# Fewer, larger instructions for the high and low parts of the probabilities in a cross-attention kernel

## Chip, cores and metric

The kernel runs on 1 core of one Trainium2 chip. The metric is device time in microseconds (us), from launch to end, of one execution. The kernel before took a median of 1032.5 us over 3 runs (1031.4, 1032.5 and 1037.69 us). The profiled execution is a further one.

## What is computed

Four batches of 2048 tokens with 640 channels attend to 77 context rows of 1024 numbers: the first 73 are text (T = 73), the last 4 are image-prompt rows. There are 20 heads of 32 channels. The reference, cut to what matters:

```python
q = heads(hidden_states @ W_q)
scores_t = jnp.einsum('bhsd,bhtd->bhst', q, k_t) * attn_scale
probs_t = jax.nn.softmax(scores_t, axis=-1)
text_out = jnp.einsum('bhst,bhtd->bhsd', probs_t, v_t)
attn_scores = jnp.einsum('bhsd,bhnd->bhsn', q, k_ip) * attn_scale
qsem = _l2norm(jnp.einsum('bhst,bte->bhse', probs_t, text_ehs))
sem = jnp.einsum('bhse,bne->bhsn', qsem, ip_n)
probs_ip = jax.nn.softmax(attn_scores + 0.5 * sem, axis=-1) * spatial_mask
ip_out = jnp.einsum('bhsn,bhnd->bhsd', probs_ip, v_ip)
out = (text_out + ip_out) @ W_out + b_out + residual
```

## The kernel before

A prologue prepares weights and per-batch tables (about the first 90 us). Then `main_loop` runs over 160 **pairs**. A pair is 256 tokens (2 blocks of 128, index j) of one group of 4 heads (HG = 4). Two pairs make a slot (512 tokens, 4 heads), five slots make a tile (512 tokens, all 20 heads), and there are 16 tiles. Each engine has its own loop over p, written out by hand; the engines meet only at semaphores. Within step p:

- TensorE (PE): the scores of pair p into `ps_S` (L1122); at times transposes of x for a later tile into `ps_M` (L1138); pieces of the output projection of the tile before into `ps_O` (L1164, the table `OUT_AT`); the product of the probabilities of pair p - 2 (LU = 2) with the table `xm` into `ps_U` (L1184), which needs the transposed probabilities `pts`; a part of the query projection of a later slot into `ps_Q` (L1198).
- VectorE (DVE): the maximum of the scores (`smax`, L1014), a copy of the image-prompt scores (`s_ip`, L1017), the exponent's bias (`bias`, L1021), low parts of queries and x (L994), then the work on pair p - 2: norms, reciprocals, `attn` (L1046 to L1102). It adds the output projection to x (L1006).
- ScalarE (ACT): copies out of PSUM (`qT` L868, `xT` L874), `at16` (L896), then for pair p eight exponentials of 73 columns (`pr`, L905), and the **high parts** (L917).
- GpSimd (POOL): three Newton steps every second pair (L944 to L950), the low part of the attention output (`at16`, L961), mask and weights of the image-prompt part (L969, L976), and the **low parts** of pair p (L987), last in its step.
- SyncE's queue (SP): in step p first the loads of tables (`kbd` L785, `xm` L795) and stores and loads of x (L801, L807), then the two DMA transposes of pair p (L825), then that of a slot's attention output (L841). All of these stand in one queue, in this order.

The probabilities go to the matmul of L1184 as two float16 numbers, a high part hi = f16(p) and a low part lo = f16(p - hi), that lie side by side as contraction rows. For each head `ph` has 256 columns: hi in 0 to 72, lo in 73 to 145, hi once more in 146 to 218 (the third piece meets the low part of the other operand), the rest is zero. Seen as `[P, 2, HG, 2, P]`, this is two tiles of 128 columns, and the low parts cross the border between them: SPLIT = 55 of them lie in the first tile, LO_B = 18 in the second. So before, ScalarE writes hi with two instructions for each j (`for col in (0, P + LO_B)`, 4 heads x 73 = 292 elements each), the semaphore `ph_ready` rises with the second, and GpSimd makes lo with two subtractions, of 4 x 55 = 220 and of 4 x 18 = 72 elements. `pl_ready` counts these: 4 for each pair. The transposes (L825) wait for `ph_ready` and `pl_ready`; so does the VectorE product (L1060), which overwrites `pr`.

`ph` and `pts` have rings of 2, `pr` one of 3. ScalarE waits before it writes `ph` until the transpose of pair p - 2 has landed; the transposes of pair p wait (L821) until TensorE has read `pts` of pair p - 2.

Of the kernel before, what the change touches and what calls it, by code (L numbers as in the profile page):

```python
# [9 lines left out]
ALU = mybir.AluOpType  # L10
ACT = mybir.ActivationFunctionType
# [7 lines left out]
HG = 4  # L19
# [604 lines left out]
def main_loop(nc, top, g):  # L624

    P, B, S, C, T, T_ALL, CC = (g[k] for k in "P B S C T T_ALL CC".split())
    XW, COL_G, COL_ONE, COL_V, IPR, HALF, DH, SPLIT = (
        g[k] for k in "XW COL_G COL_ONE COL_V IPR HALF DH SPLIT".split())
# [11 lines left out]
    X_RING, XT_RING, AT_RING, P_RING, SIP_RING, PH_RING, PT_RING = NI, 8, 10, 3, 3, 2, 2  # L640
# [4 lines left out]
    LO_B = T - SPLIT  # L645
# [9 lines left out]
    def sb(name, shape, dt):  # L655
        return top.enter_context(nc.sbuf_tensor(name, shape, dt))

    def sem(name):
        return top.enter_context(nc.semaphore(name))
# [10 lines left out]
    pr = [sb(f"pr{i}", [P, 2, HG, T], F32) for i in range(P_RING)]  # L670
    ph = [sb(f"ph{i}", [P, 2, HG, 2, P], F16) for i in range(PH_RING)]
# [23 lines left out]
    p_ready, ph_ready, pl_ready = sem("p_ready"), sem("ph_ready"), sem("pl_ready")  # L695
# [28 lines left out]
    def pair_of(p):  # L724
        return p if 0 <= p < PAIRS else None

    def slot_of(n):
        return n // 2 if n % 2 == 0 and 0 <= n // 2 < ALL_SLOTS else None

    def q_at(p):  # L730

        part = (p + 1) % 2
        m = slot_of(p + 3 - part)
        return None if m is None else (m, part)

    def x_at(p):

        if p == FIRST:
            return [(0, c) for c in range(CC)]
        return [(j, c) for at, c in XT_AT.items() for j in range(1, TILES) if STEPS * j + at == p]  # L740

    def x_bank(j, c):
        return ps_M if j else g["x_bank0"][c]
# [6 lines left out]
    def ip_at(p):  # L750

        i, at = divmod(p - IP_AT, STEPS)
        return i - 1 if at == 0 and 0 <= i - 1 < TILES else None

    def ring(sems, n):
        return sems[n % len(sems)], 16 * (n // len(sems) + 1)
# [4 lines left out]
    with nc.Block() as block:  # L761
        @block.sync
        def _(sp):
# [11 lines left out]
            for p in range(FIRST, LAST):  # L775
# [42 lines left out]
                if pair_of(p) is not None:  # L818

                    if p >= PT_RING:  # L820
                        sp.wait_ge(u_ready, p - PT_RING + 1)  # L821
                    for j in range(2):
                        sp.wait_ge(ph_ready, 2 * p + j + 1)
                        sp.wait_ge(pl_ready, 4 * p + 2 * (j + 1))
                        sp.dma_start_transpose(pts[p % PT_RING][:, j],  # L825
                                               ph[p % PH_RING][:, j].rearrange("p h k c -> p (h k c)")
                                               ).then_inc(pts_loaded[j][p % PT_RING], 16)
# [15 lines left out]
                for b in range(B):  # L843
                    if p == 2 * SLOTS * b + VW_AT:

                        one, n = vw[b % VW_RING], IPR - IP_LO
# [11 lines left out]
        @block.scalar  # L858
        def _(act):
            for p in range(FIRST, LAST):  # L860

                done = q_at(p - 1)
                if done is not None and done[1] == 1:
                    m = done[0]
                    act.wait_ge(q_ready, m + 1)
                    if m >= 2:
                        act.wait_ge(s_ready, 2 * (m - 1))
                    nc.scalar.activation(qT[m % 2][0][:], ps_Q[:], ACT.Copy).then_inc(q_hi, 1)  # L868
                for j, c in x_at(p):
                    act.wait_ge(xT_ready, CC * j + c + 1)  # L870
                    n = CC * j + c
                    if n >= XT_RING:
                        act.wait_ge(q_ready, CC * ((n - XT_RING) // CC + 1))
                    nc.scalar.activation(xT[n % XT_RING][0][:], x_bank(j, c)[:], ACT.Copy).then_inc(xT_hi, 1)  # L874
                i = ip_at(p)
                if i is not None:
                    act.wait_ge(pip_ready, CC * (i + 1))
                    if i >= 1:
                        act.wait_ge(*ring(ipT_loaded, i - 1))
                    else:  # L880
                        act.wait_ge(ones_set, 1)
                    for dst in (ip16[:, :, 0, 0:IPR], ip16[:, :, 1, IPR - IP_LO:2 * IPR - IP_LO]):
                        last = nc.scalar.activation(dst, pip[:], ACT.Copy)
                    last.then_inc(ip_hi, 1)
                m = slot_of(p - 6)
                if m is not None:

                    act.wait_ge(f_ready, m + 1)
                    nc.scalar.activation(f[:], f[:], ACT.Exp, scale=SCALE).then_inc(ef_ready, 1)
                m = slot_of(p - 4)  # L890
                if m is not None:

                    act.wait_ge(attn_ready, 2 * (m + 1))
                    if m >= 2:
                        act.wait_ge(*ring(aT_loaded, m - 2))
                    nc.scalar.activation(at16[m % 2][:, 0], attn[m % 2][:].rearrange("p s h d -> p s (h d)"),  # L896
                                         ACT.Copy).then_inc(at_hi, 1)
                if pair_of(p) is not None:

                    act.wait_ge(bias_ready, p + 1)  # L900
                    if p >= P_RING:
                        act.wait_ge(n2_done, p - P_RING + 1)
                    for j in range(2):
                        for h in range(HG):
                            last = nc.scalar.activation(pr[p % P_RING][:, j, h, :], sc[:, j, h, 0:T], ACT.Exp,  # L905
                                                        bias=bias[p % 2][:, j, h:h + 1], scale=SCALE)
                    last.then_inc(p_ready, 1)

                    act.wait_ge(p_ready, p + 1)
                    if p < PH_RING:  # L910
                        act.wait_ge(cleared, PH_RING)
                    for j in range(2):
                        if p >= PH_RING:
                            act.wait_ge(*ring(pts_loaded[j], p - PH_RING))
                        hi = ph[p % PH_RING][:, j].rearrange("p h k c -> p h (k c)")
                        for col in (0, P + LO_B):
                            last = nc.scalar.activation(hi[:, :, col:col + T], pr[p % P_RING][:, j], ACT.Copy)  # L917
                        last.then_inc(ph_ready, 1)

        @block.gpsimd  # L920
        def _(pool):
# [8 lines left out]
            for p in range(FIRST, LAST):  # L930
                i = ip_at(p)
                if i is not None:

                    pool.wait_ge(ip_hi, i + 1)
                    hi = ip16[:, :, 0, 0:IPR]
# [28 lines left out]
                if n is not None:  # L964

                    i, k = divmod(n, CC)
                    pool.wait_ge(rs_ready, n + 1)
                    j = i % NI
# [12 lines left out]
                if pair_of(p) is not None:  # L981

                    for j in range(2):
                        pool.wait_ge(ph_ready, 2 * p + j + 1)
                        one, full = ph[p % PH_RING][:, j], pr[p % P_RING][:, j]
                        for lo, t0, t1 in ((one[:, :, 0, T:P], 0, SPLIT), (one[:, :, 1, 0:LO_B], SPLIT, T)):
                            nc.gpsimd.tensor_tensor(lo, full[:, :, t0:t1], one[:, :, 0, t0:t1],  # L987
                                                    ALU.subtract).then_inc(pl_ready, 1)

        @block.vector  # L990
        def _(v):
# [8 lines left out]
            for p in range(FIRST, LAST):  # L1000
# [26 lines left out]
                for j, c in x_at(p):  # L1027
                    one = xT[(CC * j + c) % XT_RING]
# [8 lines left out]
                u = pair_of(p - LU)  # L1037
# [18 lines left out]
                                                   scalar=inv_eps, in1=y[:], op0=ALU.mult, op1=ALU.min).then_inc(f_step, 1)  # L1056
                if u is not None:

                    v.wait_ge(pl_ready, 4 * (u + 1))
                    nc.vector.tensor_tensor(pr[u % P_RING][:], uo[:, :, :, 0:T], pr[u % P_RING][:],  # L1060
                                            ALU.mult).then_inc(prod_done, 1)
                    v.wait_ge(nd_done, u + 1)
                    nc.vector.reciprocal(rd[un % 2][:, subs], nd[un % 2][:, subs, :, N_IP]).then_inc(rd_done, 1)
# [161 lines left out]
```

## Time and profile before

| | |
|---|---|
| time, median of 3 runs | 1032.5 us (1031.4 to 1037.69) |
| time of the profiled execution | 1031.25 us |
| its span, first to last instruction | 1029.5 us |
| around the span | 1.75 us |
| PE busy | 975.6 us (95%) |
| DVE busy | 795.9 us (77%) |
| ACT busy | 705.6 us (69%) |
| POOL busy | 640.5 us (62%) |
| 16 DMA engines, share of the main queue | 84.2% |

PE is the matmuls on TensorE, PEld its weight loads, SPq the issuing of DMAs on the SyncE queue. Busy time of a group is the time covered by at least one of its instructions, so that overlapping instructions count once; the mean is of a single instruction. A duration in the timeline of a merged row runs from the first start to the last end. "Released by" says which event ended an engine's wait.

### The profile page before, as it was taken

Reading aid. Unit: us, or ns where it says so; the run is one execution under the profiler, and the core shown is the slowest. Engines: PE = TensorE matmul, PEld = TensorE weight load, DVE = VectorE, ACT = ScalarE, POOL = GpSimd, SP = SyncE. Lnnn points to the kernel's source line nnn. Section 1 sums busy time; section 2 is a strip of 40 time slices with the busy share of each in tenths; the row PEclk is TensorE's granted clock in tenths of the full one; section 3 lists DMA queues with packets and bytes.
Section 4 is the critical chain, followed back from the end, with each engine's and each line's share of the span. In section 5 each row is a group of like instructions: output and inputs, shape, how many; then the busy total and the mean of one; then the engine's idle time right before and its main releaser. Section 6 shows DMA issues by size and latency. Waiting matters only on the chain.

```text
span 1029.5 us, 24562 instructions
## 1 busy us (share of the span) xinstructions
PE 975.6 (95%) x7604; PEld 795.8 (77%) x7604; DVE 795.9 (77%) x2401; ACT 705.6 (69%) x2315; POOL 640.5 (62%) x1899
## 2 busy tenths in 40 slices
PE   7986788999999999999999999999999999999877
PEld 5755566888878888888878888888878888888755
DVE  4375678888878787888878888878888888887861
ACT  1355678777677777768767777777777777787720
POOL 1112467777676667667666767766766677676750
PEclk9999989999999999999999999999999999999989
DMA  9845989879799998888899999888989979778852
GB/s 301 316 139 138 193 152 169 172 167 186 159 190 177 188 190 174 164 176 172 158 189 194 189 167 184 160 177 168 178 179 202 180 169 186 138 160 147 159 109 89
DMA packets 483871, 180.26 MB, mean 175 GB/s; under 512 B 449517, under 2 KB 461855, under 8 KB 483740
## 3 DMA queue, kind: packets, MB, share of 16 engines
q1 hardware_dynamic: 483708, 178.62, 84.2%
q8 instruction: 61, 1.00, 0.4%
q14 instruction: 70, 0.57, 0.2%
q10 hardware_dynamic: 32, 0.07, 0.0%
HBM read 42.34 MB, written 27.22 MB: 68 GB/s over the span
## 4 chain that ended last, share of the span: by engine, by line
PE 77%; DMA 4%; DVE 3%; SPq 3%; ACT 2%; issue 2%; POOL 1%; POOLq 0%; DVEq 0%; ACTq 0%
PE ps_O L1164 26%; PE ps_Q L1198 25%; PE ps_S L1122 12%; PE ps_U L1184 11%; DMA pts<-ph 3%; PE ps_M L1138 3%; ACT pr L905 1%; SPq L825 1%; SPq L795 1%; DMA x_in<-in_x_dram 1%; SPq L785 0%; DVE pr L1060 0%; DVE n L1072 0%; POOL ph L987 0%; DVE w_sem L1055 0%
## 5 line engine op out<-in xcount | busy, mean ns | idle before, releaser
L987 POOL TENSOR_TENSOR ph<-pr,ph 128x220 f16<-128x220 f32 (+1 forms) x640 | 273.8, 459 | 136.5 <-ACT ph L917 136.2
L905 ACT ACTIVATE pr<-ps_S,bias 128x73 f32<-128x73 f32 x1280 | 290.1, 339 | 89.0 <-DVE bias L1021 87.0
L1164 PE MATMUL ps_O<-wo_hi,aT 128*128 128x320 f16 x1280 | 295.1, 302 | 5.6 <-DVE x_in L1006 3.5
L1198 PE MATMUL ps_Q<-xT,wq_hi 128*128 128x512 f32 x800 | 280.6, 416 | 5.9 <-DVE qT L994 5.7
L917 ACT ACTIVATE ph<-pr 128x292 f16<-128x292 f32 x640 | 234.2, 440 | 5.5 <-DMA pts<-ph 0.4
L1164 PE MATMUL ps_O<-wo_lo,aT 128*128 128x320 f16 x640 | 192.7, 301 | 0.0
L1184 PE MATMUL ps_U<-xm,pts 128*128 128x110 f16 (+1 forms) x2560 | 159.5, 213 | 17.9 <-DMA pts<-ph 15.4
L1198 PEld LDWEIGHTS ps_Q<-xT,wq_hi 128*128 128x128 f32 x800 | 146.5, 191 | 33.6 <-DVE qT L994 7.0
L1184 PEld LDWEIGHTS ps_U<-xm,pts 128*128 128x128 f16 (+1 forms) x2560 | 145.1, 98 | 34.9 <-issue 12.4
L1164 PEld LDWEIGHTS ps_O<-wo_hi,aT 128*128 128x128 f16 x1280 | 125.7, 98 | 57.4 <-DVE x_in L1006 4.0
L1122 PEld LDWEIGHTS ps_S<-kbd,qT 128*128 128x128 f32 x960 | 149.9, 189 | 23.2 <-issue 9.2
L1122 PE MATMUL ps_S<-kbd,qT 128*128 128x308 f32 x960 | 162.7, 305 | 5.2 <-ACT pr L905 5.0
L1198 PE MATMUL ps_Q<-xT,wq_lo 128*128 128x512 f32 x400 | 159.6, 399 | 0.0
L1014 DVE TENSOR_REDUCE smax<-ps_S 128x8 f32<-128x584 f32 x160 | 121.9, 762 | 42.2 <-PE ps_S L1122 40.7
L1072 DVE TENSOR_REDUCE n<-pr 128x8 f32<-128x584 f32 x160 | 121.0, 756 | 0.0
L1060 DVE TENSOR_TENSOR pr<-ps_U,pr 128x584 f32<-128x584 f32 x160 | 117.1, 732 | 0.0
L1046 DVE COPY nd<-ps_U 128x40 f32<-128x40 f32 x160 | 31.6, 197 | 109.9 <-PE ps_U L1184 109.5
L944 POOL TENSOR_TENSOR yt<-y 128x16 f32<-128x16 f32 x240 | 51.5, 215 | 86.0 <-DVE y L1102 73.4
L961 POOL TENSOR_TENSOR at<-attn,at 128x512 f16<-128x512 f32 x80 | 92.6, 1158 | 0.0
L874 ACT ACTIVATE xT<-ps_M 128x512 fp32r<-128x512 f32 x76 | 45.2, 594 | 68.2 <-PE ps_M L1138 67.8
L1198 PEld LDWEIGHTS ps_Q<-xT,wq_lo 128*128 128x128 f32 x400 | 76.4, 191 | 14.7
L1006 DVE SCALAR_TENSOR_TENSOR x_in<-ps_O,inv,x_in 128x320 f32<-128x320 f32 x128 | 69.6, 544 | 18.1 <-PE ps_O L1164 18.1
(185 smaller groups left out, 1235.3 us busy)
## 6 DMA issues: line engine op xcount, KB each, us to landing
out_dram<-x_in SPq DMA_DIRECT2D x64, 320.0 KB, 2.6
x_in<-in_x_dram SPq DMA_DIRECT2D x56, 320.0 KB, 3.2
pts<-ph SPq DMA_TRANSPOSE x320, 3.3
aT<-in_L_xattn_W_k_dram SPq DMA_DIRECT2D x5, 512.0 KB, 8.7
w_ip<-in_L_xattn_W_k_ip_dram SPq DMA_DIRECT2D x1, 2560.0 KB, 11.6
w_v<-in_L_xattn_W_v_dram SPq DMA_DIRECT2D x1, 2560.0 KB, 18.9
w_ip<-in_L_xattn_W_v_ip_dram SPq DMA_DIRECT2D x1, 2560.0 KB, 9.3
x_in<-in_x_dram SPq DMA_DIRECT2D x2, 1280.0 KB, 12.2
```

Of the source, the lines that this page charges most:

```text
L905: last = nc.scalar.activation(pr[p % P_RING][:, j, h, :], sc[:, j, h, 0:T], ACT.Exp, bias=bias[p % 2][:, j, h:h + 1], scale=SCALE)
L917: last = nc.scalar.activation(hi[:, :, col:col + T], pr[p % P_RING][:, j], ACT.Copy)
L961: nc.gpsimd.tensor_tensor(at16[m % 2][:, 1], attn[m % 2][:].rearrange("p s h d -> p s (h d)"), at16[m % 2][:, 0], ALU.subtract).then_inc(a ...
L987: nc.gpsimd.tensor_tensor(lo, full[:, :, t0:t1], one[:, :, 0, t0:t1], ALU.subtract).then_inc(pl_ready, 1)
L1006: nc.vector.scalar_tensor_tensor(out=dst, in0=o_bank[half % 2][:, 0:HALF], scalar=inv_out, in1=dst, op0=ALU.mult, op1=ALU.add).then_inc(o_ ...
L1014: nc.vector.tensor_reduce(smax[p % 2][:], sc[:, :, :, 0:T], AX.X, ALU.max).then_inc(max_done, 1)
L1060: nc.vector.tensor_tensor(pr[u % P_RING][:], uo[:, :, :, 0:T], pr[u % P_RING][:], ALU.mult).then_inc(prod_done, 1)
L1072: nc.vector.tensor_reduce(n2[un % 2][:, subs], pr[u % P_RING][:], AX.X, ALU.add).then_inc(n2_done, 1)
L1122: last = nc.tensor.matmul(g["ps_S"][j][:, 0:GK], qT[slot % 2][a][:, q * P:(q + 1) * P], kbd[:, m, slot % CC, :], start=(a, m) == PASSES[0] ...
L1164: last = nc.tensor.matmul(o_bank[half % 2][:, 0:HALF], stationary, moving, start=(k, a, b_) == O_MMS[0], stop=(k, a, b_) == O_MMS[-1])
L1184: last = nc.tensor.matmul(uo[:, j, h, :], pts[u % PT_RING][0:n, j, 2 * h + tile, :], xm[0:n, tile, k0 * HG + h, :], start=tile == 0, stop= ...
L1198: last = nc.tensor.matmul(ps_Q[:], wq[a][:, c, k * P:(k + 1) * P], xT[(CC * i + c) % XT_RING][b_][:], start=(c, a, b_) == Q_MMS[0], stop=( ...
```

## The change

For each j ScalarE now writes both copies of the high parts with one instruction: the output pattern has a further dimension of 2 with a step of 2 x 73 columns, and the input is read twice by a step of zero in that place. GpSimd makes the 73 low parts of each head with one subtraction over columns 73 to 145, seen without the border between the tiles. `pl_ready` rises twice for each pair instead of four times, and the two waits on it are adapted. The values are the same, and so is the order of everything else. SyncE's, VectorE's and TensorE's instructions are unchanged.

```diff
@@ SyncE, before the transpose of L825
-                        sp.wait_ge(pl_ready, 4 * p + 2 * (j + 1))
+                        sp.wait_ge(pl_ready, 2 * p + j + 1)
@@ ScalarE
-                        hi = ph[p % PH_RING][:, j].rearrange("p h k c -> p h (k c)")
-                        for col in (0, P + LO_B):
-                            last = nc.scalar.activation(hi[:, :, col:col + T], pr[p % P_RING][:, j], ACT.Copy)
-                        last.then_inc(ph_ready, 1)
+                        one = ph[p % PH_RING][:, j].rearrange("p h k c -> p h (k c)")
+                        (row, _), (head, _), _ = one.ap
+                        both = bass.AP(tensor=one.tensor, offset=one.offset, ap=[[row, P], [head, HG], [2 * T, 2], [1, T]])
+                        nc.scalar.activation(both, pr[p % P_RING][:, j].unsqueeze(2).to_broadcast([P, HG, 2, T]),
+                                             ACT.Copy).then_inc(ph_ready, 1)
@@ GpSimd
-                        one, full = ph[p % PH_RING][:, j], pr[p % P_RING][:, j]
-                        for lo, t0, t1 in ((one[:, :, 0, T:P], 0, SPLIT), (one[:, :, 1, 0:LO_B], SPLIT, T)):
-                            nc.gpsimd.tensor_tensor(lo, full[:, :, t0:t1], one[:, :, 0, t0:t1],
-                                                    ALU.subtract).then_inc(pl_ready, 1)
+                        flat = ph[p % PH_RING][:, j].rearrange("p h k c -> p h (k c)")
+                        nc.gpsimd.tensor_tensor(flat[:, :, T:2 * T], pr[p % P_RING][:, j], flat[:, :, 0:T],
+                                                ALU.subtract).then_inc(pl_ready, 1)
@@ VectorE, before the product of L1060
-                    v.wait_ge(pl_ready, 4 * (u + 1))
+                    v.wait_ge(pl_ready, 2 * (u + 1))
```

ScalarE in two steps of the loop before (the numbers behind the names are those of the ring's buffers):

```order
L905 ACTIVATE pr0<-ps_S,bias0 128x73 x8
L917 ACTIVATE ph0<-pr0 128x4x73 x4
L868 ACTIVATE qT1_0<-ps_Q 128x512
L905 ACTIVATE pr1<-ps_S,bias1 128x73 x8
L917 ACTIVATE ph1<-pr1 128x4x73 x4
```

and the same place of the changed kernel, whose line numbers are 2 higher from here on:

```order
L905 ACTIVATE pr0<-ps_S,bias0 128x73 x8
L919 ACTIVATE ph0<-pr0 128x4x2x73 x2
L868 ACTIVATE qT1_0<-ps_Q 128x512
L905 ACTIVATE pr1<-ps_S,bias1 128x73 x8
L919 ACTIVATE ph1<-pr1 128x4x2x73 x2
```

Where four copies of 4 x 73 stood in a step, two of 4 x 2 x 73 stand, behind the same exponentials and ahead of the same copy of `qT`.

GpSimd before, in two steps of the loop with the subtraction for `at16` between them:

```order
L976 TENSOR_TENSOR pip<-f,se 128x4x16
L987 TENSOR_TENSOR ph0<-pr2,ph0 128x4x55
L987 TENSOR_TENSOR ph0<-pr2,ph0 128x4x18
L987 TENSOR_TENSOR ph0<-pr2,ph0 128x4x55
L987 TENSOR_TENSOR ph0<-pr2,ph0 128x4x18
L961 TENSOR_TENSOR at16_1<-attn1,at16_1 128x512
L987 TENSOR_TENSOR ph1<-pr0,ph1 128x4x55
L987 TENSOR_TENSOR ph1<-pr0,ph1 128x4x18
L987 TENSOR_TENSOR ph1<-pr0,ph1 128x4x55
L987 TENSOR_TENSOR ph1<-pr0,ph1 128x4x18
```

and now:

```order
L978 TENSOR_TENSOR pip<-f,se 128x4x16
L989 TENSOR_TENSOR ph0<-pr2,ph0 128x4x73 x2
L963 TENSOR_TENSOR at16_1<-attn1,at16_1 128x512
L989 TENSOR_TENSOR ph1<-pr0,ph1 128x4x73 x2
L946 TENSOR_TENSOR yt<-y 128x16
```

The two subtractions of a step take the place of four, and the subtraction for `at16` follows behind two instructions, not four.

## Rows read from the trace of the kernel before

**Rows 1.** The page, parts 1 and 2: busy us (share), instructions; 40 slices.

```profile
span 1029.5 us, 24562 instructions
PE 975.6 (95%) x7604; PEld 795.8 (77%) x7604; DVE 795.9 (77%) x2401; ACT 705.6 (69%) x2315; POOL 640.5 (62%) x1899
...
PE   7986788999999999999999999999999999999877
```

**Rows 2.** Windows, by stage: stretch, length, busy us of each engine, clock, DMA share.

```profile
90.00:150.00 60.00, 45.23 (x296) 36.54 (x295) 35.93 (x102) 39.29 (x132) 27.35 (x79) 0.91 0.89 172
...
350.00:550.00 200.00, 197.91 (x1610) 164.93 (x1609) 166.00 (x509) 150.54 (x507) 138.12 (x416) 1.00 0.88 173
```

**Rows 3.** Windows with L1021 (bias) alone: one instruction for each pair.

```profile
350.00:550.00 200.00, 8.94 (x36) 1.00 0.88 173
```

**Rows 4.** Waits of 85 to 180 us: total, times, longest.

```profile
PE ps_U L1184 <- DMA pts<-ph: 11.8, 13, 3.3
```

**Rows 5.** Chain of waits, 104 to 133 and 525 to 532 us: start, us, what.

```profile
108.31 1.72 POOL ph L987 x4
...
120.18 1.93 PE ps_Q L1198 x8
...
127.04 4.69 DMA pts<-ph
...
132.68 3.54 PE ps_Q L1198 x8
...
527.76 3.67 DMA pts<-ph
```

**Rows 6.** The page, part 6: DMA issues, median us to landing.

```profile
pts<-ph SPq DMA_TRANSPOSE x320, 3.3
```

**Rows 7.** Groups by line and shape: count, busy us, mean ns, idle before.

```profile
L917 ACT ACTIVATE ph<-pr 128x292 f16<-128x292 f32 x640 | 234.2, 440 | 5.5 <-DMA pts<-ph 0.4
L987 POOL TENSOR_TENSOR ph<-pr,ph 128x220 f16<-128x220 f32 x320 | 189.6, 592 | 136.5 <-ACT ph L917 136.2
...
L987 POOL TENSOR_TENSOR ph<-pr,ph 128x72 f16<-128x72 f32 x320 | 103.9, 325 | 0.0
L961 POOL TENSOR_TENSOR at<-attn,at 128x512 f16<-128x512 f32 x80 | 92.6, 1158 | 0.0
...
L896 ACT ACTIVATE at<-attn 128x512 f16<-128x512 f32 x80 | 49.4, 617 | 2.2 <-DVE attn L1085 2.2
```

**Rows 8.** Timeline of one pair in the steady part, from 500 us.

```profile
500.29 1.81 ACT L905 ACTIVATE pr<-ps_S,bias 128x73 f32<-128x73 f32 x8 [0.71 <-DVE bias L1021]
...
502.13 1.46 ACT L917 ACTIVATE ph<-pr 128x292 f16<-128x292 f32 x4
...
503.00 1.71 POOL L987 TENSOR_TENSOR ph<-pr,ph 128x220 f16<-128x220 f32 x4 [1.66 <-ACT ph L917]
...
503.96 2.60 SPq L825 DMA_TRANSPOSE pts<-ph  x2
...
512.84 0.97 PE L1184 MATMUL ps_U<-xm,pts 128*128 128x110 f16 x16
```

**Rows 9.** Chain of waits, 147 to 185 and 550 us.

```profile
147.37 0.84 POOL ph L987 x2
...
169.99 0.80 ACT ph L917 x2
...
170.86 0.95 POOL ph L987 x2
...
550.57 0.27 ACT ph L917
```

**Rows 10.** Timeline, 547 us: a bias beside a GpSimd subtraction; then all L1021, ns.

```profile
547.15 1.16 POOL L961 TENSOR_TENSOR at<-attn,at 128x512 f16<-128x512 f32 x1
547.23 1.10 DVE L1021 TENSOR_SCALAR bias<-smax 128x8 f32<-128x8 f32 x1
...
L1021 DVE TENSOR_SCALAR bias<-smax x160: 171/172/1103, 96.7 to 980.7; 128x8 f32<-128x8 f32 x160
```

## Prediction

> **What bounds the kernel now.** I read the page's busy shares first. TensorE is busy for 975.6 us, 95% of the span; ScalarE 69% and GpSimd 62%, and in the 40 slices TensorE shows a 9 from the tenth on until near the end [rows 1]. A cheaper copy on ScalarE or a cheaper subtraction on GpSimd can therefore shorten the kernel only where TensorE waits for them. The windows say where that is. In the steady part, 350 to 550 us, TensorE is busy for 197.91 of 200 us: 2.1 us of idle time at most. In the stretch from 90 to 150 us, where the output projection has not begun and TensorE has less to do for each pair, it is busy for 45.23 of 60 us, and the granted clock is 0.91 [rows 2]. So about 15 us of idle time and a lower clock lie there.
>
> In the steady part one bias instruction is issued for each pair, 36 in 200 us [rows 3], so a pair takes 200/36 = 5.56 us. Divided in the same way, ScalarE is busy for 150.54/36 = 4.18 us of it and GpSimd for 138.12/36 = 3.84 us [rows 2]. Both have more than a microsecond to spare.
>
> What TensorE waits for comes next. Between 85 and 180 us it waits 11.8 us, in 13 waits, for the transposed probabilities, which come last in the chain exponentials, high parts, low parts, DMA transpose [rows 4]. This is the place where the change can act. The chain of waits there shows that GpSimd's subtractions are a link only now and then. At 108.31 us they are one. At 127.04 us the link is a transpose that takes 4.69 us to land [rows 5], against a median of 3.3 [rows 6]: it stands in line at the DMA engines, and nothing in this change moves that line. Behind the wait follow eight projection matmuls in 3.54 us, where the same eight took 1.93 us at 120.18 us [rows 5]: TensorE runs at its lower clock level there for a while, and this costs 1.6 us.
>
> **The change part by part.** *The copies on ScalarE.* One copy of 292 elements takes 440 ns, one of 512 elements, between the same memories and the same types, 617 ns [rows 7]. The slope is 177/220 = 0.80 ns for an element, so one of 584 takes 440 + 292 x 0.80 = 675 ns. Four copies take 1.46 us together [rows 8], so they start every (1.46 - 0.44)/3 = 0.34 us and overlap by 0.10. Two new ones take 0.675 + 0.575 = 1.25 us: 0.21 less for each pair, some 34 us of busy time over 160 pairs (705.6 becomes about 672). The bounds: 617 ns below, because there are more than 512 elements, and 880 ns above, two whole copies end to end. `ph_ready` rises with the second copy as before, now 0.675 us after the first start instead of 0.34 + 0.44 = 0.78: 0.10 us earlier for the first block of 128 tokens, 0.21 for the second.
>
> *The subtractions on GpSimd.* 220 elements take 592 ns and 72 take 325 [rows 7]: 1.80 ns for an element. One of 292 takes 592 + 72 x 1.80 = 722 ns; the slope on to the 512 elements at 1158 ns gives 732, and I take 725. Four in line take 1.71 us [rows 8], two will take about 1.41. That is 0.29 less for each pair, some 46 us in all (640.5 becomes about 594). The bounds are 592 and 1158 ns, the nearest rows with fewer and with more elements.
>
> The Trainium skill, GPSIMD Engine Reference, § 3.1 Elementwise, gives about 2.6 cycles for an element of a two-input operation on this engine at 1.2 GHz. By that slope one new subtraction would take an estimated 592 + 72 x 2.17 = 748 ns; the rows here show less for an element, and the difference decides nothing.
>
> *The transposes.* In the pair at 500 us the first transpose was issued at 503.96, right behind the first two subtractions, and the two together held the SyncE queue for 2.60 us [rows 8], 1.3 each. The first block's low parts are now ready 0.10 + (0.87 - 0.725), so 0.25 us earlier (0.87 is half of the time of the four). The second transpose stands behind the first in the queue, so it too moves by 0.25. Only where it was issued as soon as its low parts came does it gain 0.10 + 0.29, about 0.4.
>
> *What this is worth in the steady part.* The second issue starts at 503.96 + 1.3 = 505.3 and lands about 3.3 us later [rows 6], at 508.6. TensorE uses that pair from 512.84 on [rows 8]. These 4.2 us hide the gain completely; they would hide a loss of the same size too. The waits that are left in this part are mostly behind transposes issued late because loads of tables stand ahead of them in the SyncE queue, or slow to land (527.76: 3.67 us [rows 5]). I cost these at nothing. The end of the kernel waits for VectorE, GpSimd's Newton steps and the last image-prompt transpose, which this change leaves alone: nothing.
>
> *What it is worth at the start of the main loop.* Here each link counts that lies in the chain. At 108.31 us the four subtractions with their copies: 0.4 us. At 127.04 us the copies only, ahead of a line at the DMA engines: 0 to 0.1, taken as 0. At 147.37 us two subtractions of 0.84 us become one of 0.725: 0.1. At 169.99 and 170.86 us the copies fall from 0.80 to 0.675 and the subtractions from 0.95 (start to signal) to some 0.75: 0.3. At 550.57 us, in the steady part, a copy: 0.1 [rows 9]. The sum is 0.9 us, and with the small waits that the chain does not show I take 1.0. The bounds of this term: nothing below, if each time another input of the same matmul is late next (the DMA line above all), and above all of the 11.8 us [rows 4] with two low-clock stretches of 1.6 us each.
>
> The profiled execution took 1031.25 us, 1029.5 in the span and 1.75 around it. Less 1.0 that is 1030.25. The median of the three runs shown is 1032.5, 1.25 above the profiled one. Taken together the four have a median of 1031.95; less 1.0, **1031.0 us** is the forecast.
>
> **A price of a different kind.** GpSimd's instructions hold up some of VectorE's. At 547.23 us the bias took 1.10 us, where its median is 172 ns and its maximum 1103, while the subtraction for `at16` ran from 547.15 on [rows 10]; the exponentials wait for this bias. The change makes single subtractions longer (592 becomes 725 ns) but their sum shorter, and it moves all that follows them in a step, so that collisions fall in other places. The Trainium skill, SBUF — State Buffer, § Who interferes with whom, says that a VectorE instruction in a two-port mode or with two SBUF inputs and a GpSimd instruction lock one another out for a whole instruction; by that rule, the trace agrees in this row (1.10 us instead of 0.17), and a longer subtraction is a longer lock. In the steady part TensorE does not wait for it. At the start, where the loop scores, maximum, bias, exponentials, scores has no slack, it could take more than the change gives.
>
> **The rivals.**
> 1. *Hidden everywhere: no change.* The DMA line and the SyncE queue set when `pts` lands, also at the start. For it: the landing of 4.69 us [rows 5]. Against it: two places where the subtractions are links [rows 5, 9]. Time: 1032.
> 2. *The start of the loop recovers much more.* The 0.25 to 0.4 us of each of the first 15 pairs add up (4 to 5 us), shorter waits keep TensorE at the high clock level (2 x 1.6 us). For it: the clock of 0.91 with the wait of up to 3.3 us [rows 2, 4]. Against it: most links of the chain there are transposes that land slowly. Time: 1024; if all 11.8 us and both stretches went, 1017.
> 3. *Slower: the bias collides.* Some 16 pairs lie between 95 and 180 us. If each bias there waited for most of a 725 ns subtraction, 0.65 us for each pair, this would be 10.5 us less the gain of 1: 1042. It decides from the point at which more than 2 of these pairs are hit anew. Against it: GpSimd's busy time falls by 7%, so a hit becomes less likely on average. A few hits, or one more low-clock stretch: 1034 to 1036.
> 4. *The merged copy falls apart.* If ScalarE paid for each of 16 runs of 73 elements in a pair as for an exponential of 73, 1.81/8 = 0.226 us [rows 8], the copies would take 3.6 us, ScalarE 4.18 - 1.46 + 3.6 = 6.3 us for a pair, more than 5.56, and some 150 pairs would cost 0.76 us each: 1145. It decides from 1.42 us for a copy. Against it: today's copies write four runs of 73 and take 0.44 us, not 0.9. On GpSimd the slack of 1.7 us for a pair means that a subtraction would have to take over 1.7 us.
>
> **How the numbers follow.** The forecast, within 1.5 us of 1031: 0.47. Rival 1: 0.22. Rival 2: 0.13, about half of it below 1022. Rival 3: 0.15, of which 0.04 is over 1%. Rival 4: 0.03. About 1% (10 us) is what a measurement of this kernel can tell from no change. So faster 0.06, the same 0.87, slower 0.07. The range takes in the milder halves of rivals 2 and 3 and the scatter of the runs (1031.25 to 1037.69): 1025 to 1037.
>
> **What would show each step.** In the profile of the changed kernel 320 copies should take 660 to 690 ns and 320 subtractions 715 to 740 ns; ScalarE should be busy for about 672 us, GpSimd for about 594; TensorE's busy time should stay within 3 us of 975.6. In a steady pair the first transpose should be issued 1.55 to 1.6 us after the first copy starts instead of 1.83, and TensorE's use of it should not move. The waits of TensorE for `pts` between 85 and 180 us should fall from 11.8 to about 11. A copy over 1.4 us or a subtraction over 1.7 us, a steady pair that takes anything but 5.56 us, or a span that moves by more than 5 us would make the prediction wrong. If biases with 0.5 us and more become frequent before 180 us, rival 3 is at work.

## The result, and the profile after

The changed kernel is slower: a median of 1036.67 us against 1034.33, 20 runs each, ratio 1.0035 with a 95% interval of 1.0022 to 1.0049. That is 3.6 us by the ratio. The forecast was 1.0 us less than before. (With 20 runs the kernel before stands at 1034.33, above the 1031.95 from which I had started.) The median lies inside the stated range of 1025 to 1037 only because that range was wide: the change went the other way. Of the executions below, one was left out of its ratio as slow, a single one of e10 with 1226.7 us at a granted clock of 0.75.

The page of the changed kernel, busy shares and the groups that answer to [rows 1, 7]:

```profile
span 1034.9 us, 23922 instructions
PE 980.2 (95%) x7604; PEld 793.6 (77%) x7604; DVE 813.8 (79%) x2401; ACT 677.7 (65%) x1995; POOL 593.2 (57%) x1579
...
L989 POOL TENSOR_TENSOR ph<-pr,ph 128x292 f16<-128x292 f32 x320 | 226.4, 729 | 158.9 <-ACT ph L919 158.9
...
L919 ACT ACTIVATE ph<-pr 128x584 f16<-128x584 f32 x320 | 205.5, 691 | 5.3 <-DMA pts<-ph 0.2
```

ScalarE lost 28 us and GpSimd 47 us of busy time, as intended. But VectorE, of which nothing was changed, is busy for 18 us more (795.9 before). The groups by line say which of its instructions became longer. First the kernel before (mean ns behind the busy time):

```profile
L1021 DVE TENSOR_SCALAR bias<-smax 128x8 f32<-128x8 f32 x160 | 36.9, 231 | 0.0
...
L1076 DVE SCALAR_TENSOR_TENSOR f<-f,s_ip 128x64 f32<-128x64 f32 x80 | 19.9, 248 | 0.0
```

and the same two of the changed kernel:

```profile
L1023 DVE TENSOR_SCALAR bias<-smax 128x8 f32<-128x8 f32 x160 | 48.1, 301 | 0.0
...
L1078 DVE SCALAR_TENSOR_TENSOR f<-f,s_ip 128x64 f32<-128x64 f32 x80 | 28.3, 354 | 0.0
```

A third, f<-nd,w_sem (L1067, now L1069), went from 260 to 311 ns. One became shorter: f<-f,fmx (L1092, now L1094), from 271 to 228 ns.

Where TensorE pays is seen in windows of 350 to 950 us, first before, then after:

```profile
350.00:950.00 600.00, 596.10 (x4840) 495.94 (x4839) 498.06 (x1533) 452.77 (x1526) 418.59 (x1258) 1.00 0.89 173
```

```profile
350.00:950.00 600.00, 595.80 (x4793) 490.47 (x4792) 507.33 (x1526) 429.48 (x1295) 382.98 (x1031) 1.00 0.89 173
```

The first pair of numbers behind the length is the matmuls' busy time and, in brackets, their count. The busy time says nothing: 596.10 and 595.80 us. The count tells: 4793 in 600 us instead of 4840, 1.0% fewer in the same time. So the loss is in the steady part. The engine's waits name the place. The weight loads for the scores, total, times and longest, before and after:

```profile
PEld ps_S L1122 <- issue: 9.2, 12, 2.8
```

```profile
PEld ps_S L1124 <- issue: 21.9, 44, 2.7
```

32 more short waits ahead of the scores, 12.7 us more in all, so 0.4 us each. The scores of a pair wait until the exponentials of the pair before have been read out of `ps_S`.

To see which pairs are hit, I took the start of the first weight load of each pair's scores from the traces and formed the time from the pair before, the median over the tiles between pairs 20 and 150. A tile has ten pairs, 0 to 9. Seven of them differ by at most 0.12 us, or gain; pairs 3, 7 and 9 lose:

| kernel | pair 3 | pair 7 | pair 9 | sum of all ten | pairs 20 to 150 in this trace |
|---|---|---|---|---|---|
| before | 5.52 | 5.31 | 5.53 | 55.45 | 728.3 |
| after | 5.78 | 5.63 | 5.81 | 56.03 | 734.1 |

0.86 us are lost and 0.28 regained in pairs 0, 4 and 8: 0.58 us for each tile, 7.5 us in 13 tiles. (What the medians leave out, single pairs that take longer, nearly all of them beside a change of batch at pairs 40, 80 and 120, differs from trace to trace and made up for 1.7 of it here.)

VectorE's instructions in step p of its loop stand ahead of the maximum of pair p + 1, and its exponentials ahead of the scores of pair p + 2. So pair 3 answers to step 1, pair 7 to step 5, pair 9 to step 7. The durations there, before / after, in ns, medians over the same 13 tiles:

| step (pair) | bias | f<-nd,w_sem | f<-f,s_ip | f<-f,fmx |
|---|---|---|---|---|
| 1 (3) | 282 / 1000 | 178 / 172 | 234 / 539 | 336 / 225 |
| 5 (7) | 171 / 493 | 207 / 560 | 236 / 209 | 225 / 224 |
| 7 (9) | 244 / 285 | 179 / 177 | 234 / 757 | 341 / 224 |

Step 1 of one tile as timeline rows, first before: VectorE's bias and GpSimd's subtraction for `at16`, then the operation on f, then the exponentials of the next pair and the scores behind them:

```profile
714.10 0.28 DVE L1021 TENSOR_SCALAR bias<-smax 128x8 f32<-128x8 f32 x1
714.30 1.17 POOL L961 TENSOR_TENSOR at<-attn,at 128x512 f16<-128x512 f32 x1
...
717.85 0.23 DVE L1076 SCALAR_TENSOR_TENSOR f<-f,s_ip 128x64 f32<-128x64 f32 x1
...
720.77 1.82 ACT L905 ACTIVATE pr<-ps_S,bias 128x73 f32<-128x73 f32 x8 [0.50 <-DVE bias L1021]
...
722.82 0.85 PEld L1122 LDWEIGHTS ps_S<-kbd,qT 128*128 128x128 f32 x5
```

and after:

```profile
718.34 1.16 POOL L963 TENSOR_TENSOR at<-attn,at 128x512 f16<-128x512 f32 x1
718.49 1.04 DVE L1023 TENSOR_SCALAR bias<-smax 128x8 f32<-128x8 f32 x1
...
722.17 1.40 POOL L989 TENSOR_TENSOR ph<-pr,ph 128x292 f16<-128x292 f32 x2 [2.68 <-ACT ph L919]
722.43 0.54 DVE L1078 SCALAR_TENSOR_TENSOR f<-f,s_ip 128x64 f32<-128x64 f32 x1
...
725.55 1.81 ACT L905 ACTIVATE pr<-ps_S,bias 128x73 f32<-128x73 f32 x8 [0.87 <-DVE bias L1023]
...
727.47 0.87 PEld L1124 LDWEIGHTS ps_S<-kbd,qT 128*128 128x128 f32 x6 [0.29 <-issue]
```

Two things happen. The `at16` subtraction now begins 0.15 us ahead of the bias, not 0.2 us behind its start; the bias ends 0.03 us after it and takes 1.04 us, not 0.28. VectorE makes up for most of that in its idle time: the operation on f starts 3.94 us after the bias, not 3.75. It starts at 722.43 inside a subtraction that began at 722.17 and takes 722 ns. It ends at 722.97, 0.08 behind the end of that subtraction, after 0.54 us, not 0.23. The maximum stands in the same queue, the bias and the exponentials behind it, and the scores wait 0.29 us.

This holds for the whole trace of the changed kernel. All 29 biases over 350 ns end 24 to 31 ns after a GpSimd instruction does, and all 53 of the operations f<-nd,w_sem, f<-f,s_ip and f<-f,fmx over 350 ns end 77 to 86 ns after one. In the kernel before it is so for 7 and 25.

### The profile page after: what moved, and what is told of

The parts are those of the page before. It is cut to its first block, busy times and chain, and to the rows that moved or that the text cites. A ratio compares the mean times of both kernels' runs of the same rounds, so it can differ in the third digit from the quotient of the medians.

```text
span 1034.9 us, 23922 instructions
## 1 busy us (share of the span) xinstructions
PE 980.2 (95%) x7604; PEld 793.6 (77%) x7604; DVE 813.8 (79%) x2401; ACT 677.7 (65%) x1995; POOL 593.2 (57%) x1579
## 4 chain that ended last, share of the span: by engine, by line
PE 77%; DVE 4%; SPq 3%; DMA 3%; issue 2%; ACT 2%; POOL 1%; POOLq 0%; DVEq 0%
PE ps_O L1166 26%; PE ps_Q L1200 25%; PE ps_S L1124 13%; PE ps_U L1186 11%; PE ps_M L1140 3%; DMA pts<-ph 2%; ACT pr L905 2%; SPq L825 1%; SPq L785 1%; SPq L795 1%; DMA x_in<-in_x_dram 1%; DVE qT L996 0%; DVE pr L1062 0%; DVE n L1074 0%; DVE bias L1023 0%
## 5 line engine op out<-in xcount | busy, mean ns | idle before, releaser
L989 POOL TENSOR_TENSOR ph<-pr,ph 128x292 f16<-128x292 f32 x320 | 226.4, 729 | 158.9 <-ACT ph L919 158.9
L919 ACT ACTIVATE ph<-pr 128x584 f16<-128x584 f32 x320 | 205.5, 691 | 5.3 <-DMA pts<-ph 0.2
L1124 PEld LDWEIGHTS ps_S<-kbd,qT 128*128 128x128 f32 x960 | 147.8, 189 | 32.7 <-issue 21.9
L1124 PE MATMUL ps_S<-kbd,qT 128*128 128x308 f32 x960 | 164.9, 307 | 7.2 <-ACT pr L905 6.7
L1008 DVE SCALAR_TENSOR_TENSOR x_in<-ps_O,inv,x_in 128x320 f32<-128x320 f32 x128 | 69.5, 543 | 17.9 <-PE ps_O L1166 17.9
```

The lines of the kernel that those rows point to most:

```text
L919: nc.scalar.activation(both, pr[p % P_RING][:, j].unsqueeze(2).to_broadcast([P, HG, 2, T]), ACT.Copy).then_inc(ph_ready, 1)
L989: nc.gpsimd.tensor_tensor(flat[:, :, T:2 * T], pr[p % P_RING][:, j], flat[:, :, 0:T], ALU.subtract).then_inc(pl_ready, 1)
L1008: nc.vector.scalar_tensor_tensor(out=dst, in0=o_bank[half % 2][:, 0:HALF], scalar=inv_out, in1=dst, op0=ALU.mult, op1=ALU.add).then_inc(o_ ...
L1124: last = nc.tensor.matmul(g["ps_S"][j][:, 0:GK], qT[slot % 2][a][:, q * P:(q + 1) * P], kbd[:, m, slot % CC, :], start=(a, m) == PASSES[0] ...
```

## The experiments

Each of the twelve was timed beside the kernel before on the same chip: e1 to e4 on one, e5 to e8 on a second, e9 to e12 on a third. The number is the ratio to the kernel before, with its 95% interval; a mean is over all instructions of a kind, a time of a pair is the median as in the table above. Theory: the **lock**, a GpSimd instruction that runs holds up VectorE's bias and its operations on f until it ends, and one long subtraction holds them longer than two short ones. Rivals: the longer copy on ScalarE, or earlier transposes; or the mere **shift** of GpSimd's work.

**One half of the change each, and both.** e1 has ScalarE's part of the diff alone, e2 GpSimd's part with the two waits, e3 is the changed kernel on the same chip.

> The kernel before with ScalarE's merged copy alone; GpSimd still makes the low parts with two subtractions. Theory 'long lock' (one subtraction of 729 ns holds up VectorE's two-input operations on f, and through them the maximum, the bias and the exponentials, three times in a tile): GpSimd's pieces are as short as before, so the ratio to the kernel before is 0.998 to 1.001 and TensorE's weight loads for the scores keep about 12 short waits. Rival 'copy' (the longer ScalarE instruction, 691 ns, delays the exponentials or the rest of ScalarE's queue): ratio 1.003 to 1.005, as in the full change. Rival 'phase' (everything on GpSimd simply comes earlier, and collides more): GpSimd starts only 0.1 us earlier here, ratio 1.000 to 1.001.

Measured: 1.0023 (1.0006 to 1.0041). Bias mean 261 ns, f<-f,s_ip 245. Pairs 3, 7, 9: 5.61, 5.43, 5.53 us.

> The kernel before with GpSimd's merged subtraction alone; ScalarE still writes the high parts with two copies. Theory 'long lock': the whole loss is here, ratio 1.002 to 1.005, f<-f,s_ip near 350 ns on average instead of 248. Rival 'copy': ratio 0.998 to 1.000. Rival 'phase': the subtraction for at16 begins 0.3 us earlier, about as in the full change (0.34), so a ratio of 1.002 to 1.005 as well; e1 and e2 do not tell length from phase, e4 and the next runs do.

Measured: 1.0056 (1.0034 to 1.0079). Bias 325 ns, f<-f,s_ip 336. Pairs 3, 7, 9: 5.90, 5.42, 5.81 us.

> The changed kernel once more, on the same chip as the other three. All theories: ratio 1.002 to 1.005, bias mean about 300 ns, f<-f,s_ip about 354 ns, some 44 short waits of the weight loads for the scores.

Measured: 1.0081 (1.0059 to 1.0102), bias 330 ns, f<-f,s_ip 346, above the 1.002 to 1.005 expected. The subtraction makes most of the loss. The copies alone cost something too, a little above what I had expected: the biases over 350 ns rose from 7 to 22, and f<-nd,w_sem of step 1 from 178 to 504 ns, behind subtractions as short as before. So GpSimd's earlier start alone is enough for some collisions. The interval of e1 reaches 1.0041 and by itself does not exclude the rival 'copy'; the pairs do better, 55.51 us in sum against 55.45 before and 56.1 in e2. The sizes differ between sets of runs (1.0035 and 1.0081 for the same kernel).

The trace of e2 shows the effect of one held operation without any change of the kernel. The same place of two neighbouring tiles:

```profile
361.69 1.50 POOL L987 TENSOR_TENSOR ph<-pr,ph 128x292 f16<-128x292 f32 x2 [1.66 <-ACT ph L917]
...
362.39 0.21 DVE L1076 SCALAR_TENSOR_TENSOR f<-f,s_ip 128x64 f32<-128x64 f32 x1
...
417.51 1.41 POOL L987 TENSOR_TENSOR ph<-pr,ph 128x292 f16<-128x292 f32 x2 [1.66 <-ACT ph L917]
...
418.24 0.76 DVE L1076 SCALAR_TENSOR_TENSOR f<-f,s_ip 128x64 f32<-128x64 f32 x1
```

In the first the operation takes 215 ns, and the second subtraction 817, 88 more than usual: here GpSimd waits. In the second the operation takes 762 ns and the subtraction 720. Of the 13 tiles, four have the long operation (761 to 769 ns) and pair 9 takes 5.81 to 6.01 us in them; of the other nine, six take 5.52 or 5.53 us, and three are the pairs beside a change of batch. (The 5.81 given above for pair 9 of e2 is thus a median at the edge between two values.)

**The locked operations freed.** `uo` is `ps_U`, which lies in PSUM.

```diff
-nc.vector.tensor_tensor(f[:], nd[fm % 2][:].rearrange("p s h n -> p (s h) n")[:, :, 0:N_IP],
+nc.vector.tensor_tensor(f[:], uo[:, 0, 0, 0:NH * N_IP].rearrange("p (a n) -> p a n", n=N_IP),
...
-                               in1=s_ip[fm % SIP_RING][:].rearrange("p s h n -> p (s h) n"),
+                               in1=uo[:, 0, 0, 0:NH * N_IP].rearrange("p (a n) -> p a n", n=N_IP),
```

> The changed kernel, with two VectorE operations on f (L1069 and L1078) reading one of their two inputs from PSUM (64 columns of ps_U, which hold other numbers) instead of SBUF: this leaves out the weights G and the image-prompt scores in f. Number, size and place of the instructions stay. Theory 'long lock': neither of the two is held up any more (no duration over 350 ns, mean under 280 ns); the maximum in pairs 6 and 8 of a tile comes 0.3 to 0.4 us earlier, two of the three losses of a tile go, and the ratio falls to 0.999 to 1.002. Rival 'copy' or a DMA that comes earlier: the ratio stays at 1.003 to 1.005, whatever these two operations take. The bias, held up by the subtraction for at16, stays near 300 ns under all theories.

Measured: 1.0013 (0.9996 to 1.0031). The two operations, by line:

```profile
L1078 DVE SCALAR_TENSOR_TENSOR f<-f,ps_U 128x64 f32<-128x64 f32 x80 | 16.9, 211 | 0.0
L1069 DVE TENSOR_TENSOR f<-ps_U,w_sem 128x64 f32<-128x64 f32 x80 | 14.2, 178 | 0.0
```

None of the 160 takes over 225 ns, beside the same long subtractions. Pairs 7 and 9 fall to 5.25 and 5.53 us. Pair 3 stays at 5.70: in step 1 the bias still takes 975 ns, and f<-f,fmx, which keeps its two inputs in SBUF, 524.

> The kernel before, with the same two VectorE operations on f (L1067 and L1076) reading one input from PSUM: this leaves out the weights G and the image-prompt scores in f. It is the control of e4. Theory 'long lock': these operations are held up little in the kernel before (means 260 and 248 ns, 0.09 and 0.04 us over their shortest), so little is to be had, ratio 0.998 to 1.001. Rival 'the PSUM input makes any kernel faster' (e4 was then no test): ratio below 0.996.

Measured: 1.0026 (1.0006 to 1.0045), slower, which I had not expected. Its two operations on f are short as well (179 and 212 ns), but the bias rose to 300 ns with 29 over 350, and pair 3 took 5.88 us: in step 1 the bias takes 1171 ns (before: 282) and f<-f,fmx 636 (before: 336). I read this as VectorE and GpSimd meeting at other moments; no run isolates it. It rules out that the PSUM input makes any kernel faster, and it shows how much hangs on the moment at which the two meet.

**The subtraction for `at16` behind the bias.**

```diff
                     pool.wait_ge(at_hi, m + 1)
+                    pool.wait_ge(bias_ready, min(p + 1, PAIRS))
```

> The changed kernel, where GpSimd's subtraction for at16 (L963) also waits until VectorE has written the bias of the same step, so that it can't hold the bias up. Theory A (the earlier at16 alone makes the loss): bias mean falls from 300 to under 240 ns, ratio 0.999 to 1.001. Theory B (the longer low-part subtraction against the operations on f makes most of it): the bias is freed in the same way, but f<-f,s_ip stays near 350 ns and pairs 7 and 9 of a tile stay at 5.6 to 5.8 us; ratio 1.002 to 1.005. I hold B for likelier, since e4, which freed f alone, took two thirds or more of the loss away.

Measured: 1.0046 (1.003 to 1.0062), bias 234 ns, f<-f,s_ip 294, f<-nd,w_sem up from 311 to 376. Pairs 3, 7, 9: 5.72, 5.63, 5.81. Theory B: with the bias freed, the loss stays. But the run does more than free the bias. The subtraction for `at16` and those behind it come later, and in step 1 f<-nd,w_sem now takes 636 ns (172 in the changed kernel); so pair 3 keeps its loss by another hold. In step 5 the bias still takes 492 ns: there another GpSimd subtraction holds it, that of the image-prompt weights (`ip<-pip,ip`, L939).

**Both freed** (the edits of e4 and e6 together).

> The changed kernel with both f operations reading one input from PSUM (e4; it leaves out the weights G and the image-prompt scores in f) and the subtraction for at16 behind the bias (e6). Theory 'locks': all three losses of a tile go, pairs 3, 7 and 9 take 5.52, 5.3 and 5.53 us, the bias takes under 240 ns on average, and the ratio is 0.998 to 1.001, at or below that of e4 (1.0013). If something else than locks carried a part of the loss, the ratio stays above 1.002.

Measured: 1.0006 (0.9987 to 1.0025), bias 204 ns, pairs 3, 7, 9 at 5.52, 5.25, 5.53 us, and 8 waits of the weight loads for the scores, not 44. No loss is left in the medians of the pairs. (The one trace of it was of its slowest execution, 1039.23 us, with 732.3 us for pairs 20 to 150: about 11 of these are what the medians leave out, about 7 in the trace of the kernel before.)

**Shorter subtractions, as many as before.**

```diff
+for h in (0, HG // 2):
+    low = nc.gpsimd.tensor_tensor(flat[:, h:h + HG // 2, T:2 * T], pr[p % P_RING][:, j, h:h + HG // 2],
+                                  flat[:, h:h + HG // 2, 0:T], ALU.subtract)
+low.then_inc(pl_ready, 1)
```

> The changed kernel, where GpSimd makes the low parts of 128 tokens with two subtractions again, but of two heads each (2 x 73 = 146 elements), so about 460 ns each instead of one of 729; ScalarE's merged copy stays. GpSimd's work is 0.2 us more for each 128 tokens than with one subtraction, as in the kernel before. Theory 'long lock': VectorE waits at most 0.46 us instead of 0.73, f<-f,s_ip falls from 354 towards 270 ns, pair 9 of a tile returns from 5.81 to about 5.55 us, ratio 1.000 to 1.003, near that of the copies alone (1.0023). Rival 'one instruction fewer or more does not matter, the shape of 73 columns across the border does': ratio as in the full change, 1.004 to 1.008.

Measured: 1.0006 (0.9987 to 1.0025). One such subtraction takes 454 ns:

```profile
L990 POOL TENSOR_TENSOR ph<-pr,ph 128x146 f16<-128x146 f32 x640 | 270.5, 454 | 139.7 <-ACT ph L919 139.6
```

The same low parts over the same border, with 44 us more of GpSimd's time, and the loss is gone within the interval: pairs 3, 7, 9 at 5.57, 5.31, 5.53 us. VectorE is still held often, with 42 biases over 350 ns, but f<-f,s_ip takes 251 ns on average and f<-nd,w_sem at most 468. Two shorter subtractions also end later than one long one, as in the kernel before. So e9 takes back the length and the shift together. It shows that the form of the low parts is innocent, not how the loss divides between length and shift.

**Room in VectorE's queue.** The block of L1008 (addition of the output projection to x) stands behind the bias of L1023 instead of ahead of the maximum, in the changed kernel (e7) and in the kernel before (e8).

> The changed kernel, with VectorE's addition of the output projection to x (L1008) moved from before the maximum to behind the bias of the same step. The maximum then comes 0.46 us earlier in most pairs, more than the 0.3 to 0.4 us that the locks cost. If the loss reaches TensorE only by the chain VectorE queue, maximum, bias, exponentials, scores, it goes: pairs 3, 7 and 9 of a tile return to 5.3 to 5.55 us or below, ratio 0.994 to 0.999, though the locks themselves stay (f<-f,s_ip over 300 ns on average). If the loss goes another way (transposes, DMA, ScalarE), the ratio stays at 1.003 or above.

Measured: 0.9997 (0.9984 to 1.0011), with bias 331 ns and f<-f,s_ip 330, so with all the locks; pairs 3, 7, 9 at 5.52, 5.23, 5.53 us. With room ahead of the maximum the held instructions no longer reach TensorE; a gain beyond that, for which I had expected a ratio of at most 0.999, did not come. The fair comparison is with e8, which has the same move:

> The kernel before with the same move of the addition to x, to see what the move is worth by itself and whether the merged instructions are worth anything once VectorE's queue has room. Pairs 1, 3, 7 and 9 of a tile had 0.11 to 0.27 us between the last exponential and the scores, so some of them gain: ratio 0.995 to 0.999. If e7 is below e8, the change pays behind this move; the theory expects them within 0.002 of each other.

Measured: 0.9988 (0.997 to 1.0006). Its ten pairs take 55.46 us in sum, e7's 55.47, and the two ratios, 0.9988 and 0.9997, lie inside each other's interval. So no other path carries a part of the loss that these runs could tell (some 2 to 3 us would be seen), and where the queue has room, 75 us less work on ScalarE and GpSimd are worth nothing that can be measured.

**SyncE's table loads behind the transposes** (the block of L785 and L795 moved behind that of L825), with the move of x, in both kernels.

> The changed kernel with the addition to x behind the bias (as in e7), and SyncE's loads of kbd and xm moved behind the transposes of the same step. In the kernel before, TensorE waits up to 2 us at the first pairs of a batch for transposes issued behind these loads. Without them 2 to 5 us go in all: ratio 0.994 to 0.998. If the time to land at those places is set by the loads' traffic and not by their place in the queue: 0.999 to 1.001.

Measured: 0.9996 (0.9973 to 1.0019).

> The kernel before with the same two moves. The difference to e10 is what the merged instructions are worth where VectorE's queue has room and the loads are out of the way: I expect 0 to 2 us in favour of e10, ratio here 0.995 to 0.999.

Measured: 0.9984 (0.9968 to 1.0001). Neither tells itself from the kernel before. The 2 to 5 us hoped for from e10 did not come, and e10 is not the faster one of the two. In the two traces pairs 20 to 150 took 727.8 and 727.2 us, the least of all, but 98.7 and 98.2 us passed before the first scores, against 94.6 in the kernel before. That stretch takes 94.0 to 99.6 us in the 14 traces, whatever the change, so one trace each is not more than a hint. No version here beats the kernel before beyond its interval.

## Why the prediction was wrong

*The prices were right.* A subtraction 725 ns forecast, 729 measured; a copy 675 against 691; GpSimd's busy time 594 against 593.2, ScalarE's 672 against 677.7. The start of the loop gave what little was expected: TensorE waits 10.1 us for `pts` between 85 and 180 us instead of 11.8 [rows 4], and from the scores of pair 0 to those of pair 20 the traces show 107.8 us against 107.3, so nothing arrived. Two signs missed: the first transpose is issued 1.70 us after the first copy starts (median over pairs 20 to 149), where I had forecast 1.55 to 1.6 and the kernel before has 1.84; and TensorE's busy time rose by 4.6 us, beyond the 3 us allowed. (One reading was off without a consequence: TensorE's slices show a 9 from the eighth on, not the tenth.)

*The step that failed* is this one: "In the steady part TensorE does not wait for it", said of the bias behind a GpSimd instruction. It rested on averages: 5.56 us for a pair, engines with a microsecond to spare, and 4.2 us between the landing of the transposes and their use. That last slack was real, and it is why the transposes played no part. But the loop has a second path to TensorE, scores, maximum, bias, exponentials, scores, and I gave it slack everywhere except at the start. The trace before shows otherwise: the exponentials of a pair end at 722.59 (720.77 + 1.82), and the next scores' weights are loaded from 722.82 on, 0.23 us later. The least that ever lies between the two is 0.11 us. By the medians over the tiles, pair 3 had 0.12 us to spare, pair 9 the same, pair 7 none, although other pairs have up to 1.5. A delay of 0.3 to 0.4 us in VectorE's queue passes through there, less the time to spare: 0.26, 0.32 and 0.28 us, three times in a tile. For pair 9 the table above gives it term by term: f<-f,s_ip takes 0.52 us more, f<-f,fmx 0.12 less, and of the 0.40 us that are left 0.12 were to spare. For pair 7, which had none, f<-nd,w_sem takes 0.35 us more and f<-f,s_ip 0.03 less.

*Rival 3* had the mechanism and the wrong place and victims. I let it act on some 16 pairs at the start and on the bias alone. It acts in every tile, and as much on f<-nd,w_sem and f<-f,s_ip, two operations that the argument never looked at. They gained 12.5 us of busy time, the bias 11.2, and pairs 7 and 9 recover when these two alone are freed (e4). The reason given against it, that GpSimd's busy time falls and a hit becomes less likely, counts the wrong thing. The longest that a hit of this kind can last grew from 592 to 729 ns, and in a loop that repeats to 0.1 us a hit is not drawn by chance. In the changed kernel one of the four instructions of the table takes over 480 ns in step 1 in all 13 tiles, in step 5 in 11, in step 7 in 12 (before: 3, 0 and 0). The rule cited, of the Trainium skill, SBUF — State Buffer, § Who interferes with whom, speaks of VectorE instructions with two SBUF inputs as well; by that rule the traces agree, down to the cure by a PSUM input in e4. I had read the rule and did not list which instructions of this kernel it names.

Rivals 1 and 2 fell with the sign of the result. Rival 4 is excluded by the 691 ns of a merged copy.

*What stays open:* why the same kernel loses 0.35% in one set of runs and 0.81% in another; the 0.58 us of a tile would be 9.3 us in 16 tiles, 0.9%, more than either. A part may be regained at the changes of batch: what the medians leave out in pairs 20 to 150 is 3 to 6 us in the traces of the changed kernel, e2, e3 and e6, and 6 to 11 in the other ten; one trace each, so a hint and not shown. Open too is how the loss of e1 (1.0023, lower end 1.0006) divides between shifted collisions and anything else in the copies, since its pairs sum to only 0.06 us a tile more than before (55.51 against 55.45); and how the whole loss divides between the longer hold and the earlier start.

## What to carry to other kernels

Merging GpSimd instructions saves their fixed cost, lengthens the time for which each can hold up the VectorE instruction beside it, and moves where the two meet: list the VectorE instructions with two SBUF inputs, and small ones like a bias, and see what is queued behind them. Slack is to be read at each wait of a repeating loop, not from a mean over it: here three pairs in ten had 0.0 to 0.12 us. And when TensorE is "busy" for 99%, count its instructions in a window; in this trace the busy time hid 1% fewer of them.

## What the runs showed of the hardware

- A VectorE instruction that GpSimd holds up ends shortly after the GpSimd instruction: the `tensor_scalar` on 8 columns (f32) 24 to 31 ns after it, operations on 64 columns with two inputs in SBUF 77 to 86 ns after it (all 29 and 53 of those over 350 ns in the changed kernel). Their recorded durations hold the wait, so a longer mean of an unchanged VectorE instruction is the sign to look for.
- The hold depends on the operands: with one input in PSUM none of 160 operations took over 225 ns (e4), with both in SBUF up to 768 ns (the changed kernel).
- It goes both ways. Where f<-f,s_ip ran in 215 ns in e2, the subtraction beside it took 817 ns, not 729. In both kinds of case the subtraction's recorded start lies 21 to 45 ns ahead of the operation's, so the record does not show which of the two will wait.
- A merged ScalarE copy of 584 elements took 691 ns, 0.86 ns for each element beyond the 292 that took 440. Reading the input twice by a zero step cost little if anything: 675 ns were forecast from copies without it.
